# A recurrence and six local-attention layers on one core: when the rows of the ffn are copied and turned, and where the merged weights are made

## What is computed

```python
x = x + attn(layernorm(x))            # h = tanh(h @ A.T + xb_t); y = h @ C.T; layernorm of (y + x)
t = layernorm(x)
for i in range(6):
    t = attn_layer(shift_tokens(t), Wqkv[i], q_scale[i], k_scale[i], Wo[i]) + t
    t = ffn_layer(shift_tokens(t), ln_g[i], ln_b[i], W1[i], b1[i], W2[i], b2[i]) + t
x = x + t
# attn_layer: q, k, v of 16 heads x 64; q, k l2-normalised, scaled, rotary; windows of 32 tokens
#             that look at their own and the window before; softmax(8 q k); (p @ v) @ Wo
# ffn_layer:  xn = layernorm(t) * g + b; a, gate = split(xn @ W1 + b1); (a * gelu(gate)) @ W2 + b2
```

## Time and profile before

| | us |
|---|---|
| median of 3 runs | 3455.07 (3452.42 to 3457.12) |
| the profiled execution | 3451.7 |
| its span, first to last instruction | 3449.9 |
| granted TensorE clock, mean | 0.989 |

### The profile page before, as it was taken

The page is one execution under the profiler, slowest core; times in us unless marked ns, Lnnn a source line. Parts: engine busy times, 40 slices in busy tenths (PEclk is TensorE's granted clock), DMA queues, the critical chain, the costliest instruction groups (busy, mean ns, idle before and its releaser), DMA issues. The chain is left out here.

```text
span 3449.9 us, 100942 instructions
## 1 busy us (share of the span) xinstructions
PE 3313.6 (96%) x42197; PEld 2155.7 (62%) x42197; DVE 2796.1 (81%) x4511; ACT 2308.7 (67%) x4545; POOL 2259.3 (65%) x1364
## 2 busy tenths in 40 slices
PE   8999689999999999999999999999999999999996
PEld 5555366666666666666666666666666666666663
DVE  2333698988898899898889889988888898988892
ACT  2222367777777777777777777777777777777774
POOL 0000476777777777777777677776777776777772
PEclk9999899999999999999999999999999999999998
DMA  2000000100001000001000001000001000000000
GB/s 72 1 1 1 7 11 9 36 11 11 8 17 35 11 8 11 11 17 33 11 11 11 8 17 35 11 9 10 11 17 32 11 11 11 12 13 17 14 8 13
DMA packets 62281, 52.50 MB, mean 15 GB/s; under 512 B 11526, under 2 KB 59396, under 8 KB 61828
## 3 DMA queue, kind: packets, MB, share of 16 engines
q1 hardware_dynamic: 61828, 46.05, 5.1%
HBM read 43.93 MB, written 2.10 MB: 13 GB/s over the span
## 5 line engine op out<-in xcount | busy, mean ns | idle before, releaser
L448 POOL TENSOR_TENSOR cosp<-cosp,rr 128x1024 f32<-128x1024 f32 x384 | 723.2, 1905 | 587.0 <-DVE rr L978 586.9
L458 POOL TENSOR_TENSOR cosp<-cosp,sinp 128x1024 f32<-128x1024 f32 x384 | 903.4, 2375 | 53.9 <-DVE sinp L957 53.7
L552 PE MATMUL ps<-w_qk,xs 128*128 128x512 f32 x1536 | 762.5, 619 | 21.0 <-ACT sq L769 17.2
L654 PEld LDWEIGHTS ps<-px,w_vo 128*128 128x128 f32 x6144 | 701.0, 192 | 57.5 <-ACT px L822 44.2
L654 PE MATMUL ps<-px,w_vo 128*128 128x128 f32 x6144 | 721.6, 276 | 2.0 <-ACT px L822 1.7
L769 ACT ACTIVATE sq<-ps 128x1024 f32<-128x1024 f32 x384 | 393.0, 1023 | 473.5 <-DVE sinp L957 473.5
L954 DVE TENSOR_TENSOR cosp<-ps,tab 128x1024 f32<-128x1024 f32 x384 | 469.2, 1222 | 143.0 <-PE ps L552 141.6
L552 PEld LDWEIGHTS ps<-w_qk,xs 128*128 128x128 f32 x1536 | 262.9, 191 | 385.9 <-issue 376.0
L963 DVE TENSOR_REDUCE ss<-sq 128x16 f32<-128x1024 f32 x384 | 455.2, 1185 | 55.0 <-ACT sq L769 54.9
L957 DVE TENSOR_TENSOR sinp<-ps,tab 128x1024 f32<-128x1024 f32 x384 | 465.9, 1213 | 0.0
L714 PE MATMUL ps<-pT,xtm 32*128 32x512 f32 x3072 | 447.6, 625 | 12.7 <-issue 5.5
(11 more groups left out here) (106 smaller groups left out, 4502.4 us busy)
## 6 DMA issues: line engine op xcount, KB each, us to landing
tab<-in_tab SPq DMA_DIRECT2D x96, 128.0 KB, 2.1
qks<-in_scales SPq DMA_DIRECT2D x96, 128.0 KB, 3.4
w_qk<-in_L_ffn_Wqkv SPq DMA_DIRECT2D x12, 512.0 KB, 6.0
w_v<-in_wv_t SPq DMA_DIRECT2D x6, 512.0 KB, 7.4
w_o<-in_L_ffn_Wo SPq DMA_DIRECT2D x6, 512.0 KB, 8.5
x<-in_L_attn_x SPq DMA_DIRECT2D x16, 128.0 KB, 4.7
out<-w_v SPq DMA_DIRECT2D x16, 128.0 KB, 2.5
w<-in_L_ffn_W SPq DMA_DIRECT2D x6, 341.0 KB
```

The lines of the kernel that those rows point to most:

```text
L448: eng.tensor_tensor(v, v, rr[:, B % 2, HEADS * i:HEADS * i + HEADS].unsqueeze(2).to_broadcast([P, HEADS, DH]), ALU.mult).then_inc(rot_read ...
L458: eng.tensor_tensor(cosp[:, A % 2, i, :], cosp[:, A % 2, i, :], sinp[:, i, :], ALU.add).then_inc(rot_added, 1)
L552: t = eng.matmul(ps[:, u, :], xs[:, n % ROUND, :], w_qk[:, n // TILES % 2, i, 512 * u:512 * u + 512], start=True, stop=True)
L654: t = eng.matmul(Y, w_vo[:, i // HP, i % HP, :], px[:, i, :], start=i == 0, stop=i == HEADS - 1)
```

## The change

1. **Merged weights in parts.** w_vo becomes double. From layer 1 on the 16 products are made as four parts of four in the value steps 16, 20, 24, 28 of the layer before (`fuse_of`), each before the product with w_vo and into banks 5 and 6; ScalarE copies a part out behind exp, and the q turn waits for that. Layer 0's parts go into the recurrence, chunks 3 to 6 at step 24, in place of a warming matmul; VectorE copies them. The loads are issued one turn sooner.
2. **Rows early.** In the rows' step ScalarE copies xr directly behind the kT copies, and VectorE's statistics read xr in place of PSUM. POOL makes the variance before it scales the next table.
3. **Two value products in the rows' step.** m = 1 moves there from the value step, into bank 4 (G(0)).
4. **Normalised rows one step sooner.** xn is written in the value step between exp and the square, turned back behind that step's value product, and xf is copied before the second square. Before, it was turned and copied in the product step.
5. xe takes the place of w_o at the end of the program, to make room for the second w_vo.

```diff
-AT_OUTPUT, AT_INPUT, AT_XN, AT_START = 3, 38, 46, 58
+AT_OUTPUT, AT_FUSE, AT_INPUT, AT_XN, AT_START = 3, 24, 38, 46, 58
...
-        w_vo = sb("w_vo", [P, 2, HP, D])
+        w_vo = sb("w_vo", [P, 2, 2, HP, D])
...
-        xe = sb("xe", [P, CH])
...
+        xe = w_o.rearrange("p k d -> p (k d)")[:, 0:CH]
...
-        def layer_of(s):
-            L = (s - 2) // TILES
-            return L if (s - 2) % TILES == 0 and 0 <= L < DEPTH else None
+        def fuse_of(s):
+            L, part = s // TILES + 1, s % TILES // ROUND - 4
+            return (L, part) if s % ROUND == 0 and part >= 0 and L < DEPTH else None
...
-        VALUES = ((11, 0, 2), (12, 1, 1), (12, 2, 2))
+        VALUES = ((11, 0, 2), (11, 1, 0), (12, 2, 2))
...
-                if L + 1 < DEPTH and T % NC == 3:
+                if L + 1 < DEPTH and T % NC == 2:
                     load_qk(L + 1)
                     load_vo(L + 1)
...
-                    if A % ROUND == 1:
-                        scale_table(1, A // ROUND)
-                    if A % ROUND == 3 and A + 1 < NT:
-                        scale_table(0, A // ROUND + 1)
                 T = turn_of(s, 7)
                 if T is not None:
...
+                if tile(A):
+                    if A % ROUND == 1:
+                        scale_table(1, A // ROUND)
+                    if A % ROUND == 3 and A + 1 < NT:
+                        scale_table(0, A // ROUND + 1)
...
+            def fuse(L, part):
+                if part == 0:
+                    eng.wait_ge(wv_in, 16 * (L + 1))
+                    eng.wait_ge(wo_in, 16 * (L + 1))
+                if L == 0:
+                    after(eng, vo_evac, part)
+                for i in range(2 * part, 2 * part + 2):
+                    for x in range(2):
+                        rows = slice(64 * x, 64 * x + 64)
+                        t = eng.matmul(ps[:, 5 + x if L else 2 + 4 * x, D * (i % 2):D * (i % 2) + D], w_v[rows, i, :], w_o[rows, i, :], start=True, stop=True)
+                t.then_inc(vo_done, 1)
...
+                    elif t == AT_FUSE and c - 3 in range(4):
+                        fuse(0, c - 3)
...
-                T = turn_of(s, 9)
-                if T is not None:
-                    eng.wait_ge(xn_ready, TB * (T + 1))
-                    evacuated(s, 1)
-                    for i in range(TB):
-                        t = eng.transpose(G(1)[:, P * i:P * i + P], xn[:, i, :], ident[:, :])
-                    t.then_inc(cols_done, 1)
...
+                T = turn_of(s, 8)
+                if T is not None:
+                    eng.wait_ge(xn_ready, TB * (T + 1))
+                    evacuated(s, 1)
+                    for i in range(TB):
+                        t = eng.transpose(G(1)[:, P * i:P * i + P], xn[:, i, :], ident[:, :])
+                    t.then_inc(cols_done, 1)
...
-                T = turn_of(s, 9)
+                T = turn_of(s, 8)
...
                 if tile(E):
                     eng.wait_ge(px_evac, 3 * (E + 1))
                     eng.wait_ge(px_last, E + 1)
+                    if fuse_of(s):
+                        fuse(*fuse_of(s))
                     if E % TILES == 0:
                         eng.wait_ge(vo_evac, 4 * (E // TILES + 1))
                     after(eng, y_added, E)
                     for i in range(HEADS):
-                        t = eng.matmul(Y, w_vo[:, i // HP, i % HP, :], px[:, i, :], start=i == 0, stop=i == HEADS - 1)
+                        t = eng.matmul(Y, w_vo[:, E // TILES % 2, i // HP, i % HP, :], px[:, i, :], start=i == 0, stop=i == HEADS - 1)
                     t.then_inc(y_done, 1)
...
-                L = layer_of(s)
-                if L is not None:
...
-                    for i in range(HP):
-                        for x in range(2):
-                            t = eng.matmul(G(2 * x + i // 4)[:, D * (i % 4):D * (i % 4) + D], w_v[64 * x:64 * x + 64, i, :],
-                                           w_o[64 * x:64 * x + 64, i, :], start=True, stop=True)
-                            if i % 4 == 3:
-                                t.then_inc(vo_done, 1)
...
                 if tile(B):
-                    if L is not None:
-                        eng.wait_ge(vo_evac, 4 * (L + 1))
+                    if fuse_of(s):
+                        L, part = fuse_of(s)
+                        eng.wait_ge(vo_evac, 4 * L + part + 1)
                     eng.wait_ge(rot_ready, 2 * B + 1)
                     turn(B, 0, Q_BANKS)
...
-                T = turn_of(s, 7)
-                if T is not None:
-                    eng.wait_ge(stat_step, 2 * TB * T + TB)
-                    after(eng, xn_ready, TB * T)
-                    eng.copy(xr[:, :, :].rearrange("p j d -> p (j d)"), G(1)).then_inc(rows_evac, 1)
...
-                T = turn_of(s, 8)
-                if T is not None:
-                    eng.wait_ge(shift_done, T + 1)
-                    eng.wait_ge(rows_evac, T + 1)
-                    after(eng, cols_done, T)
-                    for i in range(TB):
-                        at = 2 * HEADS + i
-                        eng.activation(xn[:, i, :], xr[:, i, :], ACT.Identity, bias=shift[:, i:i + 1], scale=rr[:, 1, at:at + 1]).then_inc(xn_ready, 1)
...
-                T = turn_of(s, 9)
-                if T is not None:
-                    eng.wait_ge(ln_in, 32 * (T // NC + 1))
-                    eng.wait_ge(cols_done, T + 1)
-                    after(eng, a_done, 3 * T)
-                    eng.activation(xf[:, :], G(1), ACT.Identity, bias=vec[:, 1:2], scale=vec[:, 0:1]).then_inc(affine_done, 1)
...
+                if fuse_of(s):
+                    L, part = fuse_of(s)
+                    eng.wait_ge(vo_done, 4 * L + part + 1)
+                    after(eng, y_done, TILES * (L - 1))
+                    eng.copy(w_vo[:, L % 2, :, 2 * part:2 * part + 2, :], ps[:, 5:7, 0:2 * D].rearrange("p x (i d) -> p x i d", d=D)).then_inc(vo_evac, 1)
+                T = turn_of(s, 8)
+                if T is not None:
+                    eng.wait_ge(shift_done, T + 1)
+                    eng.wait_ge(rows_evac, T + 1)
+                    after(eng, cols_done, T)
+                    for i in range(TB):
+                        at = 2 * HEADS + i
+                        eng.activation(xn[:, i, :], xr[:, i, :], ACT.Identity, bias=shift[:, i:i + 1], scale=rr[:, 1, at:at + 1]).then_inc(xn_ready, 1)
...
-                L = layer_of(s)
-                if L is not None:
-                    for k in (0, 2, 1, 3):
-                        eng.wait_ge(vo_done, 4 * L + (2 if k % 2 == 0 else 4))
-                        eng.copy(w_vo[:, k // 2, 4 * (k % 2):4 * (k % 2) + 4, :].rearrange("p i d -> p (i d)"), G(k)).then_inc(vo_evac, 1)
...
+                T = turn_of(s, 7)
+                if T is not None:
+                    eng.wait_ge(rows_done, T + 1)
+                    after(eng, xn_ready, TB * T)
+                    eng.copy(xr[:, :, :].rearrange("p j d -> p (j d)"), G(1)).then_inc(rows_evac, 1)
...
                         value(T, m, k)
+                T = turn_of(s, 8)
+                if T is not None:
+                    eng.wait_ge(ln_in, 32 * (T // NC + 1))
+                    eng.wait_ge(cols_done, T + 1)
+                    after(eng, a_done, 3 * T)
+                    eng.activation(xf[:, :], G(1), ACT.Identity, bias=vec[:, 1:2], scale=vec[:, 0:1]).then_inc(affine_done, 1)
...
+                if c - 3 in range(4):
+                    part = c - 3
+                    eng.wait_ge(vo_done, part + 1)
+                    for x in range(2):
+                        t = eng.tensor_copy(w_vo[:, 0, x, 2 * part:2 * part + 2, :].rearrange("p i d -> p (i d)"), ps[:, 2 + 4 * x, 0:2 * D])
+                    t.then_inc(vo_evac, 1)
                 normalise(c + 1)
...
             last = Steps(eng, post_step, (NC - 1) * POST_STEPS)
@@ -979,10 +993,10 @@
 
             def statistics(T):
                 base = 2 * TB * T
-                eng.wait_ge(rows_done, T + 1)
+                eng.wait_ge(rows_evac, T + 1)
                 after(eng, stat_step, base)
                 for i in range(TB):
-                    eng.bn_stats(stat[:, i, :], G(1)[:, P * i:P * i + P]).then_inc(stat_step, 1)
+                    eng.bn_stats(stat[:, i, :], xr[:, i, :]).then_inc(stat_step, 1)
                 after(eng, variance_done, 2 * T)
                 for i in range(TB):
                     eng.wait_ge(stat_step, base + i + 1)
```

## The result

| | before | after |
|---|---|---|
| median us (range) | 3456.1 (3452.42 to 3465.97), 4 runs | 3423.38 (3418.59 to 3425.97), 4 runs |
| the profiled execution, its span | 3451.7, 3449.9 | 3425.0, 3422.8 |
| busy us of PE, PEld, DVE, ACT | 3313.6, 2155.7, 2796.1, 2308.7 | 3293.5, 2147.5, 2802.8, 2306.9 |

The ratio after to before is 0.9899, 95% interval 0.988 to 0.9917: faster by 1.0%, 7 us above the forecast of 3416 and inside its range. The two profiled executions lie 27 us apart, the medians 33.

A forecast was written before the change was run, and what follows sets the result against it. VectorE, with the places where engines wait for each other, was taken to bound the round, not PE. Rounds 11.5, merged weights 25.6 and tail 2.0 make 39.1 us off 3451.7, 3412.6; the median lies 3.4 higher: 3416 us, range 3386 to 3445.

The forecast's parts named there:

- The round: Four steps: rows' step +0.37, value step -0.19, product step -0.43, together -0.25 us; 46 rounds give -11.5 us.
- the walk: ScalarE's chain in the rows' step, followed copy by copy: square at 1234.94 for 1234.02, VectorE +0.37 us.
- the second rival: Rows' step: square 0.55 us later still, as the very last kT copy frees bank 4; 3441 us, chance 0.20.
- The parts: Twenty in value steps: L654 0.9 later, some 0.5 us spare, so 0.4 each, +8.0 us (2 to 24).
- The pieces: Merged weights made whole in gate steps: five inner ones at 5.90 us go, 29.5 us saved.
- The first piece: Step 2: without it the second projection waits only for the square; -6.1 us.
- The recurrence: Takes layer 0's four parts, one each in four chunks, for a warming matmul: +2.0 us (0 to 4).
- The tail: Last two turns, chain uncovered: transposes and a value product made a step sooner give -2 us (0 to -4).
- rivals at 3432 and 3441: 3432: a part costs 1.2 us, chance 0.10; 3441: rows' step square 0.55 us later still, chance 0.20.
- PE carries the round: Rows' step: PE's stall would come back whole, 1.1 us a round, 51 for 11.5, so 3376 us; chance 0.10.
- the parts cost what the pieces did: Value steps: at 1.2 us a part, 24 of the 29.5 us come back; 3432 us, chance 0.10.
- the two longer chains: ScalarE, rows' step: square 0.55 us later, 3441, chance 0.20; or late roots, px and xn copies, 3474, chance 0.05.

The follow-up runs named there:

- parts_only: Kernel before with only the merged weights made in parts; value products, rows and normalised rows as before: 3434.74 us, ratio 0.992.
- sq_first: Changed kernel with ScalarE making the square before the second value copy in the rows' step: 3426.84 us, ratio 0.9897.
- row_copy_only: Kernel before with ScalarE's row copy behind the kT copies, statistics reading xr, variance ahead of the table product: 3446.89 us, ratio 0.9965.

## Why the prediction was right, point by point

- **The round.** Forecast +0.37 - 0.19 - 0.43 = -0.25, measured -0.24. Counted from the start of the kT copies in the rows' step, the walk had the first value copy at 1.51 and the square at 2.95; they came at 1.61 and 3.01. The square sum was to wait 0.65 for it and idled 0.62. Counted from the start of the rows' step, PE's second projection in the value step came 22.17 us later for 21.79 before: +0.38 for +0.35. From there to the end of the product step -0.62 was forecast, and 23.92 us became 23.30. By the medians of all undisturbed steps the round is -0.20. It is spread otherwise than I said: at the value step's end PE is 0.34 sooner and VectorE 0.19, so the next step begins with PE ahead, its second projection idles a little longer for the square, and the product step shows -0.30 and not -0.43.
- **Bank 4.** The second value product starts 1.24 us behind the start of the kT copies, where the walk had it, and 0.14 behind the end of the last of them; against the stream's 0.43 it is held up by 0.04. L721 starts 0.98 later in the step where 0.86 was forecast. The square is 0.06 behind the walk and not 0.55, so the second rival fell.
- **The parts** are the mis-sized term: 0.4 each was forecast, 0.13 to 0.17 measured, at most 3.4 us for 8.0. A part puts L672 0.74 and not 0.9 later, and the cover is 0.58 and not 0.5: each error is small, but the term is their difference. That the cover is the late square's doing, as the forecast had it, parts_only shows (0.68 a part), and sq_first too (0.65).
- **The pieces.** Forecast 29.5, measured 30.6. The first piece lay in step 2: 21.42 to 16.55, -4.9, with step 1 0.95 longer, so some -3.9; I had -6.1. **The recurrence** +1.9 for +2.0. **The tail** -3.4 for -2.
- **What the sum lacked** are the fetch stalls, +18.9 us of gaps and some 20 us of longer steps. Without the 19.9 us that the third stretch lacks, the difference of the spans would be -47.0, 7.9 better than the forecast's 39.1: 4.6 from the parts, 1.4 from the tail, 1.1 from the pieces, 1.2 from the first 16 steps, less 0.5 in the rounds. The two errors partly cancel, and the range, drawn for other reasons (rivals at 3432 and 3441), took what was left: that part of the hit is luck. The row for it stood in the waits of before, 19.6 us of "issue" in the similarities, and no term of the prediction has it. It depends on where the code lies and on what PE waits for beside it. The clock has no term either: the one piece of before in whose step it fell cost 7.26 us, the others 5.49 to 6.42.
- **The rivals.** "PE carries the round" fell with row_copy_only, "the parts cost what the pieces did" with 0.17 a part, and the two longer chains with the 0.62 us wait and the xn copies, which end ahead of sinp (the square idles 0.34 in the step without a part, 0.21 with one).

## What to carry to other kernels

A stall of the busiest engine is worth only the slack of the engine that comes second: 1.13 us taken from PE brought 0.31, because VectorE had no more to give, and the slack could be read beforehand from one px copy. In this kernel, work moved into small parts was nearly free as long as each part stayed inside a wait that was there anyway, and cost its full records from that point on. A wait that is taken away may have covered something else: the stall of step 79 cost 0.98 us with the wait for xr and 2.07 without. When every regular step is as forecast and the total is not, compare the waits for "issue" line by line, and shift the code before you explain them by the change.

## What the runs showed of the hardware

- TensorE, with all operands there, stood still for 0.4 to 3.1 us inside bursts of 256 short instructions in 1.4 us. The places repeat from execution to execution, three steps apart over long stretches, and move when 32 small matmuls are added in the recurrence. There are 11 to 31 such stalls, 22.6 to 44.7 us in a program of 3,440, in the fourteen traces, and 34.4 and 41.5 us in two executions of one program. 32 small matmuls alone made before 0.25% slower (0.1 to 0.4), partly by the clock.
- The code comes in packets of 16,384 bytes, of which each takes 1.1 us, for 252 matmul and load instructions. All 334 stalls of the fourteen traces end 1.1 to 1.6 us behind the end of a packet, so they are waits for code. When a packet is asked for, and why after has more such waits, was not shown.
- In the steps at full load TensorE's clock fell from 2.4 to 1.2 GHz for 3.4 to 10.2 us at a time, 65 times in fourteen traces, in 64 of them 1.0 to 4.4 us after the start of an idle time of 1.3 to 2.9 us.
- A change between 64-row and 128-row operands costs TensorE at most some 0.15 us, an estimate from 0.74 us for a part of eight records and 0.45 us for eight more of them.
